# Closings without GpSimd's drain, an earlier gate batch, and experts' weights ahead of the last store

## The chip, the cores and the metric

The kernel runs on one core of a Trainium2 chip, as one program. A core has a matrix engine (TensorE, PE), a vector engine (VectorE, DVE), a scalar engine (ScalarE, ACT), a general one (GpSimd, POOL) and SyncE (SP), which here only issues transfers. The engines run side by side, each in its own order, and wait for one another through semaphores. The metric is the time of one execution on the device, in microseconds, as the median of three runs.

## What is computed

The input `x` is 2 sequences of 4096 tokens with 256 numbers each. Three parts follow one another, each on the result of the last:

```python
x = x + 0.5 * ffn(layernorm(x))        # part one
x = x + attention(layernorm(x))        # part two
x = x + 0.5 * ffn(layernorm(x))        # part three

def ffn(x):                            # 8 experts, each token goes to its best 2
    scores = softmax(x @ gate_w)                       # gate_w: 256 x 8
    scale = the two largest scores of a token, 0 for the other six
    xs = scale.T[:, :, None] * x[None]
    h = silu(xs @ w1[e]) * (xs @ w3[e])                # 256 -> 128
    return sum over e of h @ w2[e]                     # 128 -> 256

def attention(x):                      # 4 heads of 64, chunks of 64 tokens
    q, k, v = silu(causal convolution of x @ Wq, Wk, Wv, 4 taps); q, k normalized
    per chunk: T = inverse(I + strictly lower part of (beta k) k^T)
               mid = T (beta v) - T (beta k) S^T
               out = q S^T + lower part of (q k^T) mid;   S = S + mid^T k
    return (rms norm of out) @ Wo
```

## The kernel before

There are three blocks, one for each part (`ffn`, `attention`, `ffn`). A block holds one program for each engine. At its end all five engines meet, `clear_semaphores` sets the block's semaphores to zero on GpSimd and lets all engines meet once more, and the next block starts.

**How a feed-forward part works.** Each token's row is written twice into a table in memory, `first_rows`, once in each chosen expert's list. Where in a list it goes is its position: how many earlier tokens chose the same expert. GpSimd writes the rows, 128 at a time, by indirect transfers ("scatters"). Then the lists are read in tiles of 128 rows, multiplied with the expert's weights, and scattered again. Part three has no gate of its own: its gate, the positions, the table of tiles and the first scatters are done inside attention, and so is the loading of the experts' weights (`load_weights`: five transfers on SyncE's queue into `raw_w`, 3 MB). ScalarE and VectorE split these into a high part (L2120, eight instructions) and a low part (L1885, eight instructions) before the block ends.

**How attention works.** It takes 32 steps, each of 128 tokens of both sequences, in a pipeline that is written out by hand: `steps_of` calls each engine's `body(f, g, t, s, u, v)`, in which `f`, `g`, `t`, `s` and `u` are the step that is at the front, at the inverses, at their completion, at the state and output, and at the gate. A step's result is added to the residual `xres` (L1653, which raises `y_read`), stored by SyncE (`store_result`), and its gate products are taken. Four steps make one gate batch `v[0]` of 8 tiles; there are 8 batches, 0 to 7. A batch goes through its stages while `v[1]` is 1, 2, 3 and then 0:

- `gate_pow` on GpSimd (L2148, L2151), which needs the statistics of the batch's last result (`gmv_ready`);
- `gate_norm`, `gate_first`, `gate_second`, `gate_sums` on VectorE (to L1743), which choose the experts;
- `positions` on TensorE (L1373 to L1377), three products that count them;
- `gate_scores`, `gate_row_ends`, `gate_ends`, `gate_places` on VectorE (L1749 to L1789), which make each row's scores and places;
- `load_batch` on SyncE, which reads the batch's rows back from `x_after_attention` into the one buffer `xg`, once they are stored and the batch before is scattered;
- `gate_scatter` on GpSimd (L2159), eight scatters.

Batch 6 is in the stage `v[1] == 3` while step 31, the last, is at its state and output. Batch 7 needs step 31's result and runs after it. When its places are known, VectorE works out the table of tiles (`work_out`) and then the weights' low parts. The lines around the change that set the order on SyncE, VectorE and GpSimd:

```python
hold(stored, 64 * (n + 1)); hold(gscattered, 16 * GB * n)   # load_batch
hold(sq_ready, NS); hold(mid_done[h], NS)                   # load_weights
wait(dve, gscattered, 16 * GB * n)                          # gate_row_ends
pool.wait_ge(grow_part, ...); pool.wait_ge(grow_made, ...); pool.wait_ge(xg_loaded, ...)   # gate_scatter
pool.wait_ge(gmv_ready, 4 * (n + 1))                        # gate_pow
hold(gscattered, 16 * NT)                                   # SyncE, last thing in attention
```

## Time and profile before

| | us |
|---|---|
| three runs | 1544.03, 1541.20, 1538.71 |
| median | 1541.2 |
| the profiled execution's own time | 1542.23 |
| its span (first to last instruction) | 1540.5 |
| part one, to attention's first instruction | 394.6 |
| attention, to part three's first instruction | 890.2 |
| part three | 255.7 |

The span is what the profile shows; the profiled execution took 1.7 us more than that. The three parts' lengths are the distances between the first instructions of SyncE's queue in each (at 394.57 and 1284.79 us). The profile gives for each engine the busy time, and for each instruction its start, its length and what ended the idle time before it. An instruction that is busy on an engine that nobody waits for costs nothing.

### The profile page before, as it was taken

How to read it: one execution, taken by the hardware profiler on the slowest of the kernel's cores; microseconds unless marked ns; L12 is line 12 of the kernel's file. 1: busy time of each engine (PE TensorE's matmuls, PEld its weight loads, DVE VectorE, ACT ScalarE, POOL GpSimd, SP SyncE). 2: the span in 40 equal slices, each digit the busy share in tenths (PEclk: the TensorE clock that was granted, in tenths of full speed). 3: DMA queues.
4: the chain of work that ended last, by engine and by line, in shares of the span. 5: the costliest groups of instructions: out<-in, count | busy, mean ns of one | idle time of the engine just before them, and what ended most of it. 6: DMA issues, size and time to landing. Idle time of an engine off the chain costs nothing. (4 is left out here: it accounts for less than half of the span.)

```text
span 1540.5 us, 38923 instructions
## 1 busy us (share of the span) xinstructions
PE 1281.9 (83%) x12840; PEld 1176.3 (76%) x12840; DVE 1083.6 (70%) x2722; ACT 954.4 (62%) x1948; POOL 965.6 (63%) x1716
## 2 busy tenths in 40 slices
PE   6763995898369999999999999999999723994996
PEld 6662995898358888888888888888888623994996
DVE  6574673576467788889888898898887452773674
ACT  2123672774257787788778787787776423772773
POOL 4773565377246566678777786776867431674466
PEclk7665998899679999999999999999999856997999
DMA  7436984774011121232222322223222265875682
GB/s 216 159 105 175 299 268 167 262 271 140 21 20 42 44 52 44 50 92 65 77 61 62 86 64 81 66 59 83 59 79 57 72 193 166 270 252 210 240 287 73
DMA packets 224034, 196.04 MB, mean 127 GB/s; under 512 B 105556, under 2 KB 186714, under 8 KB 223840
## 3 DMA queue, kind: packets, MB, share of 16 engines
q1 hardware_dynamic: 190560, 117.21, 27.7%
q0 software_dynamic: 24576, 67.94, 12.1%
q10 hardware_dynamic: 8704, 8.39, 1.8%
q8 instruction: 111, 1.82, 0.5%
q14 instruction: 83, 0.68, 0.2%
HBM read 103.68 MB, written 96.10 MB: 130 GB/s over the span
## 5 line engine op out<-in xcount | busy, mean ns | idle before, releaser
L1552 DVE SCALAR_TENSOR_TENSOR raw_w<-attn_raw,taps,raw_w 128x256 f32<-128x256 f32 x576 | 246.2, 490 | 30.0 <-ACT raw_w L1934 29.9
L468 PE MATMUL ffn_both<-ws,ffn_xhi 128*128 x1152 | 204.6, 290 | 0.7 <-issue 0.2
L457 PE MATMUL ffn_both<-ident,ffn_xb 128*128 128x128 f32 x576 | 82.1, 290 | 103.1 <-ACT ffn_xb L753 103.1
L468 PEld LDWEIGHTS ffn_both<-ws,ffn_xhi 128*128 128x128 f32 x1152 | 165.1, 193 | 3.2 <-issue 3.2
L2219 POOL TENSOR_TENSOR attn_inv<-attn_inv,attn_term 64x14 f32<-64x14 f32 (+6 forms) x448 | 132.7, 296 | 35.1
L457 PEld LDWEIGHTS ffn_both<-ident,ffn_xb 128*128 128x128 f32 x576 | 70.0, 149 | 105.5 <-ACT ffn_xb L753 83.6
L2216 POOL TENSOR_TENSOR attn_term<-attn_small,attn_inv 64x14 f32<-64x14 f32 (+6 forms) x448 | 125.0, 279 | 32.6
L1204 PE MATMUL attn_fr<-attn_xhi,wqkv 128*128 128x256 f32 x768 | 139.2, 291 | 3.6 <-ACT attn_bth L1941 2.0
L491 PE MATMUL ffn_yb<-ws,ffn_hhi 128*128 x576 | 118.7, 290 | 6.5 <-DVE ffn_hlo L667 6.2
L1204 PEld LDWEIGHTS attn_fr<-attn_xhi,wqkv 128*128 128x128 f32 x768 | 109.7, 193 | 15.2 <-issue 10.6
L468 PE MATMUL ffn_both<-ws,ffn_xlo 128*128 x576 | 116.3, 284 | 0.0
L830 POOL DMA_INDIRECT second_rows<-ffn_more_rows,ffn_to x64 | 63.1, 985 | 84.7 <-DVE ffn_to L652 68.8
L753 ACT ACTIVATE ffn_xb<-ffn_more_rows 128x256 f32<-128x256 f32 x120 | 62.1, 591 | 85.9 <-DMA ffn_more_rows<-first_rows 50.8
L657 DVE TENSOR_TENSOR ffn_xlo<-ffn_both,ffn_xhi 128x1024 fp32r<-128x1024 f32 x72 | 87.7, 1219 | 37.1 <-ACT ffn_xhi L760 37.1
L662 DVE TENSOR_TENSOR ffn_hid<-ffn_both,ffn_sil 128x512 f32<-128x512 f32 x72 | 49.8, 691 | 89.2 <-ACT ffn_sil L765 89.2
L765 ACT ACTIVATE ffn_sil<-ffn_both 128x512 f32<-128x512 f32 x72 | 43.0, 597 | 91.5 <-PE ffn_both L468 91.5
L491 PEld LDWEIGHTS ffn_yb<-ws,ffn_hhi 128*128 128x128 f32 x576 | 93.5, 190 | 7.7 <-issue 7.7
L760 ACT ACTIVATE ffn_xhi<-ffn_both 128x1024 fp32r<-128x1024 f32 x72 | 73.9, 1026 | 34.0 <-PE ffn_both L457 34.0
L2159 POOL DMA_INDIRECT first_rows<-attn_xg,attn_slots x64 | 69.2, 1082 | 35.0 <-issue 16.5
L468 PEld LDWEIGHTS ffn_both<-ws,ffn_xlo 128*128 128x128 f32 x576 | 90.3, 192 | 0.0
L1934 ACT ACTIVATE raw_w<-attn_raw,taps 128x256 f32<-128x256 f32 x192 | 87.0, 501 | 2.0
L819 POOL DMA_INDIRECT first_rows<-ffn_xb,ffn_slots x64 | 65.5, 1023 | 36.3 <-DVE ffn_xb L642 18.1
(310 smaller groups left out, 3878.2 us busy)
## 6 DMA issues: line engine op xcount, KB each, us to landing
ffn_more_rows<-second_rows SPq DMA_DIRECT2D x56, 259.0 KB
ffn_xb<-second_rows SPq DMA_DIRECT2D x48, 259.0 KB, 4.9
raw_w<-second_rows SPq DMA_DIRECT2D x40, 259.0 KB, 4.0
ffn_more_rows<-first_rows SPq DMA_DIRECT2D x64, 131.0 KB
ffn_xb<-in_L_attn_x_dram SPq DMA_DIRECT2D x8, 1024.0 KB, 5.5
attn_xin<-x_after_first ACTq DMA_DIRECT2D x32, 256.0 KB, 2.7
attn_xres<-x_after_first SPq DMA_DIRECT2D x32, 256.0 KB, 3.0
x_after_attention<-attn_xres SPq DMA_DIRECT2D x32, 256.0 KB, 2.2
```

The source lines that it names most:

```text
L457: last = pe.transpose(tr[:, q, j * P:(j + 1) * P], xs[:, k % 2, j, q * P:(q + 1) * P], ident[:])
L468: last = pe.matmul(hp[:, j, :], (xhi, xlo)[b][:, k % 2, q, j * P:(j + 1) * P], ws[:, bass.ds(experts[j], 1), a, q].rearrange("p o d -> p ( ...
L491: last = pe.matmul(yb[:, j, :], (hhi, hlo)[b][:, k % 2, j * P:(j + 1) * P], ws[:, bass.ds(experts[j], 1), a, 2].rearrange("p o d -> p (o d)"),
L657: dve.tensor_tensor(xlo[:, k % 2], tr, xhi[:, k % 2].bitcast(F32), ALU.subtract).then_inc(xlo_ready, 1)
L760: act.activation(xhi[:, k % 2], tr, ACT.Copy).then_inc(xhi_ready, 1)
L819: pool.indirect_dma_start(out=rows1, out_offset=bass.IndirectOffsetOnAxis(ap=slots[:, m % 2, j:j + 1], axis=0), in_=xb[:, m % 4, j, :], in ...
L1204: last = pe.matmul(out, w[:, a, q, col], (xhi, xlo)[b][:, q, :], skip_group_check=True, start=(start and k == 0 and q == 0), stop=(k == 2 ...
L1552: dve.scalar_tensor_tensor(acc[:, j, r], raw[:, j, r, :, tap:tap + P], taps[:, j, r, tap:tap + 1], acc[:, j, r], ALU.mult, ALU.add)\
L1934: act.activation(acc[:, j, r], raw[:, j, r, :, 0:P], ACT.Copy, scale=taps[:, j, r, 0:1])\
L2159: pool.indirect_dma_start(out=rows1, out_offset=bass.IndirectOffsetOnAxis(ap=slots[:, j:j + 1], axis=0), in_=xg[:, j, :], in_offset=None). ...
L2216: pool.tensor_tensor(term[:, 0:k, 0:j], n[:, j + 1:, j:j + 1].broadcast_to([BP, k, j]), v[:, j:j + 1, 0:j].broadcast_to([BP, k, j]), ALU.m ...
L2219: pool.tensor_tensor(v[:, j + 1:, 0:j], v[:, j + 1:, 0:j], term[:, 0:k, 0:j], ALU.subtract)\
```

## The change

Three things are changed.

1. All blocks are opened with `no_gpsimd_drain=True`. GpSimd's `DRAIN` before the meeting at a block's end is gone, at all three blocks. What `clear_semaphores` does between blocks stays: there GpSimd still has a `DRAIN` (L96) before it clears the semaphores, and another before the second meeting (L97). After the last block there is no `clear_semaphores`.
2. Batches 6 and 7 put their counts into `fr` instead of `sc` (`counts_of`). Batch 6's positions stand first in step 31 on TensorE, its places on VectorE behind `remainder`, its load on SyncE one step earlier (`v[1] == 2`), and all its scatters on GpSimd in step 31: two ahead of `out_factor`, six behind it. Batch 7 keeps its place.
3. `load_weights` stands ahead of the last `store_result`.

In the diff the engines follow one another in this order: SyncE, TensorE, VectorE, GpSimd.

```diff
-        block = ctx.enter_context(nc.Block())
+        block = ctx.enter_context(nc.Block(no_gpsimd_drain=True))
...
+        LAST = NS // 4 - 1
+
+        def counts_of(n):
+            a, b = 2 * GB * E, 2 * (GB + 1) * E
+            place = fr[:, 0] if n >= LAST - 1 else sc[:, 1, 2 * E:]
+            return place[:, 0:a], place[:, a:b]
...
-                if v and v[1] == 3:
+                if v and v[1] == (2 if v[0] == LAST - 1 else 3):
                     load_batch(v)
+                if s and isinstance(s[0], int) and (s[0] == NS - 1):
+                    load_weights()
                 if s:
                     store_result(s)
                 if g:
                     collect_inverses(g)
                     place_inverses(g)
-                if s and isinstance(s[0], int) and (s[0] == NS - 1):
-                    load_weights()
...
             def positions(v, u):
                 n = v[0]
                 pe.wait_ge(gmask_ready, n + 1)
-                if u is None:
-                    pe.wait_ge(glg_read, NS)
...
+                if n >= LAST - 1:
+                    pe.wait_ge(vtok_ready, NS)
+                if n == LAST:
+                    pe.wait_ge(grow_part, ROWS * n - 4)
+                each, total = counts_of(n)
...
             def body(f, g, t, s, u, v):
+                if v and v[1] == 3 and v[0] == LAST - 1:
+                    positions(v, u)
                 if s:
                     state_in(s, v)
...
-                if v and v[1] == 3:
+                if v and v[1] == 3 and v[0] != LAST - 1:
                     positions(v, u)
...
             def gate_products_out(u, v):
-                if v and v[1] == 3:
+                if v and v[1] == 3 and v[0] != LAST - 1:
                     dve.wait_ge(gpos_done, v[0] + 1)
...
                 if s:
                     remainder(s)
+                if v and v[1] == 3 and v[0] == LAST - 1:
+                    gate_ends(v)
+                    gate_scores(v)
+                    gate_row_ends(v)
+                    gate_places(v)
...
-                if v and v[1] == 0:
+                if v and v[1] == 0 and v[0] < LAST - 1:
                     gate_scatter(v, 0, 3)
...
-                if v and v[1] == 1 and (v[0] > 0):
+                if v and v[1] == 1 and 0 < v[0] < LAST:
                     gate_scatter((v[0] - 1, 1), 3, 5)
-                if v and v[1] == 2 and (v[0] > 0):
+                if v and v[1] == 2 and 0 < v[0] < LAST:
                     gate_scatter((v[0] - 1, 2), 5, GB)
+                if v and v[1] == 3 and v[0] == LAST - 1:
+                    gate_scatter(v, 0, 2)
                 if s:
                     out_factor(s)
+                if v and v[1] == 3 and v[0] == LAST - 1:
+                    gate_scatter(v, 2, GB)
```

On GpSimd, from step 30's last work to the end of attention, the rows before stand like this (`ws<-ws,attn_cc` is the state's remainder scaled, `attn_og` is `out_factor`, `attn_gvar` and `attn_grstd` are batch 7's `gate_pow`; the first three scatters are batch 5's, the rest are batch 6's and 7's):

```order
L2245 TENSOR_TENSOR ws<-ws,attn_cc 128x256 x2
L2159 DMA first_rows<-attn_xg,attn_slots 67584x262 x3
L2253 TENSOR_TENSOR attn_og<-attn_osum,attn_powers 128x8
L2245 TENSOR_TENSOR ws<-ws,attn_cc 128x256 x2
L2253 TENSOR_TENSOR attn_og<-attn_osum,attn_powers 128x8
L2159 DMA first_rows<-attn_xg,attn_slots 67584x262 x3
L2148 TENSOR_SCALAR attn_gvar<-attn_gmv 128x8
L2151 TENSOR_TENSOR attn_grstd<-attn_gvar,attn_powers 128x8
L2159 DMA first_rows<-attn_xg,attn_slots 67584x262 x13
```

And in the changed kernel, in the same place:

```order
L2258 TENSOR_TENSOR ws<-ws,attn_cc 128x256 x2
L2172 DMA first_rows<-attn_xg,attn_slots 67584x262 x3
L2266 TENSOR_TENSOR attn_og<-attn_osum,attn_powers 128x8
L2258 TENSOR_TENSOR ws<-ws,attn_cc 128x256 x2
L2172 DMA first_rows<-attn_xg,attn_slots 67584x262 x2
L2266 TENSOR_TENSOR attn_og<-attn_osum,attn_powers 128x8
L2172 DMA first_rows<-attn_xg,attn_slots 67584x262 x6
L2161 TENSOR_SCALAR attn_gvar<-attn_gmv 128x8
L2164 TENSOR_TENSOR attn_grstd<-attn_gvar,attn_powers 128x8
L2172 DMA first_rows<-attn_xg,attn_slots 67584x262 x8
```

All of batch 6's scatters now stand ahead of batch 7's `gate_pow`, and two of them ahead of step 31's `out_factor`.

On SyncE's queue, from step 30's residual load on, before (`attn_xres<-x_after_first` is a residual load, `x_after_attention<-attn_xres` a store, `attn_xg<-x_after_attention` a batch's load, `raw_w<-in_L_ffn_w_dram` the weights):

```order
L1108 DMA attn_xres<-x_after_first 128x2x256
L1113 DMA x_after_attention<-attn_xres 128x2x256
L1108 DMA attn_xres<-x_after_first 128x2x256
L1120 DMA attn_xg<-x_after_attention 128x4x256 x2
L1113 DMA x_after_attention<-attn_xres 128x2x256
L196 DMA raw_w<-in_L_ffn_w_dram 128x8x128 x4
L198 DMA raw_w<-in_L_ffn_w_dram 128x8x256
L1120 DMA attn_xg<-x_after_attention 128x4x256 x2
```

And in the changed kernel:

```order
L1114 DMA attn_xres<-x_after_first 128x2x256
L1126 DMA attn_xg<-x_after_attention 128x4x256 x2
L1119 DMA x_after_attention<-attn_xres 128x2x256
L1114 DMA attn_xres<-x_after_first 128x2x256
L196 DMA raw_w<-in_L_ffn_w_dram 128x8x128 x4
L198 DMA raw_w<-in_L_ffn_w_dram 128x8x256
L1119 DMA x_after_attention<-attn_xres 128x2x256
L1126 DMA attn_xg<-x_after_attention 128x4x256 x2
```

Batch 6's load moved past one store and one residual load, and the five weight transfers moved past the last store.

On TensorE, from the gate transpose in step 31 to the gate products behind it, before (`attn_sc<-attn_picked,attn_before` and the two rows behind it are batch 6's positions, `attn_ob<-wos,attn_oT` is step 31's output projection, `attn_sc<-ident,attn_xres` a gate transpose and `attn_sc<-attn_gws,attn_gT` gate products):

```order
L1350 MATMUL attn_sc<-ident,attn_xres 128x128 x4
L1446 MATMUL attn_ob<-ident,attn_on 128x128 x4
L1455 MATMUL attn_ob<-wos,attn_oT 128x256 x4
L1362 MATMUL attn_sc<-attn_gws,attn_gT 128x8 x4
L1373 MATMUL attn_sc<-attn_picked,attn_before 128x128
L1375 MATMUL attn_sc<-attn_upto,attn_ones 128x128
L1377 MATMUL attn_sc<-attn_upto,attn_ones 128x16
L1350 MATMUL attn_sc<-ident,attn_xres 128x128 x4
L1362 MATMUL attn_sc<-attn_gws,attn_gT 128x8 x4
```

In the changed kernel these three rows stand at the start of step 31 (`attn_sc<-attn_state,ws` and `attn_ob<-attn_state,ws` are the step's products with the state):

```order
L1337 MATMUL attn_tp<-raw_w,attn_tt 64x64 x8
L1380 MATMUL attn_fr<-attn_picked,attn_before 128x128
L1382 MATMUL attn_fr<-attn_upto,attn_ones 128x128
L1384 MATMUL attn_fr<-attn_upto,attn_ones 128x16
L1399 MATMUL attn_sc<-attn_state,ws 128x128 x4
L1409 MATMUL attn_ob<-attn_state,ws 128x128 x4
```

Batch 6's positions moved ahead of everything that step 31 does on TensorE, and out of the way of step 31's gate transpose.

## Rows read from the trace of the kernel before

**Rows 1.** Stretches: span time, then each engine's busy time, clock and DMA share.
```profile
core 0: us, PE busy (x) PEld busy (x) DVE busy (x) ACT busy (x) POOL busy (x), PEclk, DMA share, GB/s
...
1243.00:1285.00 42.00, 4.09 (x27) 3.67 (x26) 22.34 (x71) 6.83 (x10) 19.65 (x18) 0.54 0.64 186
```
**Rows 2.** Timeline of GpSimd (POOL), attention's last steps: start us, length us, instruction, [idle before].
```profile
1234.00 1.64 POOL L2253 TENSOR_TENSOR attn_og<-attn_osum,attn_powers 128x8 f32<-128x8 f32 x1 [3.55 <-DVE attn_osum L1636]
...
1245.66 1.06 POOL L2159 DMA_INDIRECT first_rows<-attn_xg,attn_slots  x1 [10.02 <-DVE attn_xg L1789]
...
1249.29 0.27 POOL L2148 TENSOR_SCALAR attn_gvar<-attn_gmv 128x8 f32<-128x8 f32 x1
...
1256.76 0.96 POOL L2159 DMA_INDIRECT first_rows<-attn_xg,attn_slots  x1 [0.30 <-issue]
...
1266.18 0.96 POOL L2159 DMA_INDIRECT first_rows<-attn_xg,attn_slots  x1 [8.46 <-DMA attn_xg<-x_after_attention]
...
1277.09 0.96 POOL L2159 DMA_INDIRECT first_rows<-attn_xg,attn_slots  x1 [0.30 <-issue]
```
**Rows 3.** Timeline of VectorE (DVE), the same stretch.
```profile
1233.04 0.69 DVE L1633 TENSOR_REDUCE attn_oms<-attn_on 128x8 f32<-128x512 f32 x1 [3.40 <-ACT attn_on L2038]
...
1242.03 0.69 DVE L1653 TENSOR_TENSOR attn_xres<-attn_ob,attn_xres 128x512 f32<-128x512 f32 x1 [3.87 <-PE attn_ob L1455]
...
1243.94 0.29 DVE L1774 TENSOR_TENSOR attn_row<-attn_sc,ends 128x128 f32<-128x128 f32 x1 [1.22 <-PE attn_sc L1377]
...
1245.36 0.74 DVE L1660 BATCH_NORM_STATS2 attn_gstats<-attn_xres 128x6 f32<-128x256 f32 x2
...
1259.62 0.17 DVE L1761 TENSOR_SCALAR attn_xg<-attn_xg 128x8 f32<-128x8 f32 x1 [3.22 <-DMA first_rows<-attn_xg,attn_slots]
...
1261.13 0.17 DVE L1789 COPY attn_xg<-attn_slot 128x8 f32<-128x8 f32 x1
...
1268.53 7.03 DVE L1885 TENSOR_TENSOR ws<-raw_w,ws 128x768 fp32r<-128x768 f32 x8
```
**Rows 4.** Timeline of TensorE (PE), the same stretch.
```profile
1228.02 1.16 PE L1392 MATMUL attn_sc<-attn_state,ws 128*128 128x128 f32 x8
...
1243.09 0.47 PE L1373 MATMUL attn_sc<-attn_picked,attn_before 128*128 128x128 f32 x2
...
1256.91 0.45 PE L1377 MATMUL attn_sc<-attn_upto,attn_ones 128*128 128x16 f32 x2
```
**Rows 5.** Timeline of SyncE's queue (SPq), the same stretch.
```profile
1242.75 0.36 SPq L1113 DMA_DIRECT2D x_after_attention<-attn_xres  x1
...
1243.22 4.18 SPq L196 DMA_DIRECT2D raw_w<-in_L_ffn_w_dram  x4
...
1259.68 0.92 SPq L1120 DMA_DIRECT2D attn_xg<-x_after_attention  x2
```
**Rows 6.** Timeline of ScalarE (ACT), the same stretch.
```profile
1256.73 5.97 ACT L2120 ACTIVATE ws<-raw_w 128x768 fp32r<-128x768 f32 x8 [2.60 <-DMA raw_w<-in_L_ffn_w_dram]
```
**Rows 7.** DMA traffic from 1243 to 1257 us.
```profile
DMA packets 5748, 4.21 MB, mean 301 GB/s; under 512 B 182, under 2 KB 5558, under 8 KB 5747
```
**Rows 8.** GpSimd's drains at the closings: count, ns min/median/max, first and last start.
```profile
L893 POOLq DRAIN  x1: 14049/14049/14049, 1269.3 to 1269.3; - x1
...
L224 POOLq DRAIN  x2: 9879/9916/9953, 383.0 to 1530.4; - x2
...
L96 POOLq DRAIN  x2: 178/205/232, 393.2 to 1283.6; - x2
```
**Rows 9.** Who SyncE's queue waited for, from 1530 us on: us in total, times, longest.
```profile
SPq L224 <- PEq L224: 3.4, 1, 3.4
```
**Rows 10.** Timeline, the last scatter of part one and the first instruction of attention.
```profile
387.33 0.98 POOL L830 DMA_INDIRECT x_after_first<-raw_w,ffn_to  x1 [0.30 <-issue]
...
394.57 0.39 SPq L1180 DMA_DIRECT2D attn_gws<-in_L_ffn_gate_w_dram  x1
```
**Rows 11.** Chain that ended last, its first piece: start us, us, what.
```profile
1284.79 0.30 SPq L345
```

More of the change, by code:

```diff
@@ L1057, in attention @@
                              "gscl_ready", "gpos_done", "grow_part", "grow_made", "xg_loaded", "gscattered"))
-        block = ctx.enter_context(nc.Block())
+        block = ctx.enter_context(nc.Block(no_gpsimd_drain=True))
         x_v = src.rearrange("(s n p) d -> n p s d", s=2, p=P)
@@ L1369, in positions @@
                 pe.wait_ge(gmask_ready, n + 1)
[L1370 to L1375 removed]
+                if n >= LAST - 1:
[3 more added lines that the diff above has]
+                each, total = counts_of(n)
+                pe.matmul(each, before[:], choice.rearrange("p r j e -> p r (j e)"),
+                          start=n >= LAST - 1, stop=False, skip_group_check=True)
+                pe.matmul(each, ones[:], upto8[:, :, GB - 1:2 * GB - 1].rearrange("p r j e -> p r (j e)"),
                           start=False, stop=True, skip_group_check=True)
[L1377 removed]
+                pe.matmul(total, ones[:], upto8[:, :, 2 * GB - 1, :],
                           start=False, stop=True, skip_group_check=True).then_inc(gpos_done, 1)
@@ L1770, in gate_ends @@
                 n = v[0]
-                a, b = 2 * E + 2 * GB * E, 2 * E + 2 * (GB + 1) * E
+                each, total = counts_of(n)
                 dve.wait_ge(gpos_done, n + 1)
                 wait(dve, grow_part, ROWS * n)
-                dve.tensor_tensor(row[:], sc[:, 1, 2 * E:a].rearrange("p (r j e) -> p r j e", r=2, e=E),
+                dve.tensor_tensor(row[:], each.rearrange("p (r j e) -> p r j e", r=2, e=E),
                                   kept.ends[:].unsqueeze(2).broadcast_to([P, 2, GB, E]), ALU.add).then_inc(grow_part, 1)
                 dve.wait_ge(grow_part, ROWS * n + 1)
-                dve.tensor_tensor(kept.ends[:], kept.ends[:], sc[:, 1, a:b].rearrange("p (r e) -> p r e", r=2), ALU.add)\
+                dve.tensor_tensor(kept.ends[:], kept.ends[:], total.rearrange("p (r e) -> p r e", r=2), ALU.add)\
                    .then_inc(grow_part, 1)
@@ L1847, in body @@
                     conv(f, 2, 1, 2)
-                if v and v[1] == 3:
+                if v and v[1] == 3 and v[0] != LAST - 1:
                     gate_scores(v)
@@ L1855, in body @@
                     gate_first(v)
-                if v and v[1] == 3:
+                if v and v[1] == 3 and v[0] != LAST - 1:
                     gate_row_ends(v)
@@ L1866, in body @@
                         clear_buffers()
-                if v and v[1] == 3:
+                if v and v[1] == 3 and v[0] != LAST - 1:
                     gate_ends(v)
```

5 lines of the change are left out of this document (removed).

## Prediction

> **What bounds the kernel now.** I read the stretches first, then the timeline of each engine in the one stretch where all are slack, then the drains, and last the chain.
>
> From 1243 to 1285 us TensorE is busy for 4.1 of 42 us and no other engine for much more than half [rows 1]: this is the seam between attention and part three, and nothing there is limited by arithmetic. Its order is read from GpSimd's timeline. Step 31's result is written at 1242.03 + 0.69 = 1242.7 [rows 3]. Batch 6's places follow it, because its positions stand behind step 31's products on TensorE (1243.09, rows 4); they start at 1243.94 on VectorE [rows 3], and the first scatter of batch 6 starts at 1245.66 [rows 2]. Batch 7's `gate_pow` stands behind three of these scatters and starts at 1249.29, though the statistics it needs (0.74 us from 1245.36, and 0.25 us of aggregation) were there at 1246.4 [rows 2, 3]. The last scatter of batch 6 ends at 1257.72 and has landed at 1259.62, when VectorE goes on after 3.22 us of idle time [rows 2, 3]: 1.9 us from issue to landing. Only then can batch 7's rows be loaded into `xg` (1259.68, rows 5), and its scatters run from 1266.18 to 1277.09 + 0.96 = 1278.05, after 8.46 us of waiting for that load [rows 2]. VectorE, with the table and the weights' low parts, is done at 1268.53 + 7.03 = 1275.56 [rows 3], which is sooner. So the seam ends by this: places of batch 6, eight scatters, load, eight scatters.
>
> Then comes GpSimd's drain: it begins at 1269.3 and takes 14.05 us, so it ends at 1283.35, 5.3 us after the last scatter's issue [rows 2, 8]. Part three starts at 1284.79 [rows 11]. At the end of part one the same drain ends at 383.0 + 9.95 = 392.95, 4.6 us after the last scatter's 388.31, and attention starts at 394.57 [rows 8, 10].
>
> **The seam, batch 6.** Its positions cost 0.7 to 0.8 us on TensorE (1243.09 to the next transpose) and now stand ahead of step 31's first products at 1228.02 [rows 4]. That step is a chain from end to end, so all of it moves by +0.8. On VectorE the twelve instructions of places and scores take about 2.3 us (six of them take 1.4, from 1243.94 to the 1245.36 of the next; rows 3); they lie in the 3.40 us in which VectorE waited ahead of 1233.04 [rows 3], and hide there with 1 us to spare. If they did not fit, the excess would be added to the chain. The places are there at about 1232.8, and the rows are loaded since the step before, so the first two scatters run from 1233.1, at 1.3 us each (0.96 and an idle 0.30, rows 2), to 1235.5. `out_factor` stands behind them. It started at 1234.00 [rows 2], would now start at 1234.8, and starts at 1235.5: +0.7 more. Step 31's result is late by 1.5 us: 1244.2. This is what is paid.
>
> What is bought: the other six scatters run behind `out_factor` (ends 1237.2) while TensorE and VectorE finish step 31, 6 x 1.27 = 7.6 us, to 1244.8; landed 1246.7. The statistics of batch 7 need the result and step 30's gate products and are there at 1246.0, 0.4 us sooner than before in spite of the later result, since places no longer stand between. GpSimd is free by then, so `gate_pow` starts at 1246.1, not at 1249.29: -3.2.
>
> **The seam, batch 7.** From `gate_pow`'s start to the end of the positions it was 1249.29 to 1256.91 + 0.45 = 1257.36, 8.1 us [rows 2, 4]; so 1254.2 now. Scores hide beside the positions, and the 3.22 us wait for batch 6's landing goes, as that is over at 1246.7. What follows took 1259.62 to 1261.13 + 0.17 = 1.7 us [rows 3]: places at 1255.9, 5.4 sooner than before.
>
> The scatters also need the rows. The weights are now issued as soon as step 31's middle products are done, about 1232.1 instead of 1243.22. Before, their last byte was there at 1256.73, 13.5 us after the first issue [rows 5, 6], in a stretch that moved 4.21 MB at 301 GB/s [rows 7]. That stretch held eight scatters too, and holds them again, so I take 13.5 us: 1245.6. The last store is issued at 1244.3, finds the end of the weights ahead of it and lands at about 1247; the load of batch 7 then takes what it took, 1259.68 to 1266.18 = 6.5 us [rows 2, 5]: 1253.5, 2.4 us ahead of the places. So the places decide. Scatters start at 1256.2 and take 11.9 us as before (1266.18 to 1278.05): 1268.0.
>
> VectorE's table takes 1261.30 to 1268.53 = 7.2 and the low parts 7.03 [rows 3]: from 1255.9 to 1270.1. ScalarE's high parts, 5.97 us [rows 6], lie ahead of that. So VectorE now reaches the meeting last.
>
> The Trainium skill has a rule against this edit ("DMA: Bandwidth & Descriptors", Queues, rings and completion order): a completion's increment lands only after all earlier writes of the same transfer engine, so a store behind 3 MB of loads is reported behind them. By it the store is there after the weights, as in my sum, and it costs nothing as long as the load wins against the places.
>
> **The drain.** Between blocks GpSimd has another drain, L96, which took at most 0.23 us right behind the long one [rows 8]. What the long one waits for no row says. I bound it from both sides. If it waits for a state that comes 5.3 us (4.6 in part one) after the last scatter's issue, L96 now waits for it: 1268.0 + 5.3 = 1273.3 at the seam. From L96's end (1283.6 + 0.23) to part three's start it was 0.96 us [rows 8, 11]; so part three starts at 1274.3, 10.5 us sooner. At part one's end L96 ended at 393.4 and now ends at 392.95: -0.45. If instead the drain is a routine of 4.6 to 5.3 us that runs when it is called with scatters behind it, it starts only when all engines have met: at the seam 1270.2 + 5.3 + 0.96 = 1276.5 (-8.3), at part one's end 389.9 (some 3 us before the drain's end, where SyncE arrives, as in rows 9) + 4.6 + 1.15 = 395.7 (+1.1). If L96 costs 0.2 whatever came before, 1271.4 (-13.4) and -3.2. I take the first: it lies between the others, and it is what the long drains did, which all began before the last scatters and ended 4.6 to 5.3 us after the last issue.
>
> At part three's end nothing of the kernel follows. SyncE waited 3.4 us for the drain there [rows 9]; that less the meeting is 3.2 us off the span. Whether it is off the time depends on what lies in the 1.7 us between span (1540.5) and time (1542.23), which the trace doesn't show. Ends 0 and -3.2; nothing is nearer to either, and I take the middle, -1.6.
>
> By the Trainium skill ("Runtime: NRT & Kernel Launch", The ~15µs preamble/postamble breakdown) the runtime's own closing waits for all engines. If the time includes it and GpSimd is still held there, this term is 0 and the sum -10.95; no row shows it.
>
> Sum: -10.5 - 0.45 - 1.6 = -12.55. The profiled execution's 1542.23 becomes 1529.7. It lies 1.0 above the runs' median of 1541.2, so the forecast is 1528.6.
>
> **Rivals.**
> - *The drain goes altogether* (L96 costs 0.2): -13.4 - 3.2 - 3.2 = -19.8, 1521.4. For it: it was 0.2 us where it stood. Against: it stood behind the long one.
> - *The drain starts when called*: -8.3 + 1.1 - 1.6 = -8.8, 1532.4. For it: a scatter's bytes are there 1.9 us after issue, and the drain goes on for 3 us more. Against: nothing else.
> - *The weights hold the last batch back.* All transfers of SyncE share one queue. From the point where batch 7's rows land later than 1256.2, each microsecond of delay of the weights is one of the seam; that is weights landed later than 1248.3, 16.2 us after their first issue instead of 13.5. At 20 us it would cost 3.8: 1532.4. At 3.2 MB in 36 us (90 GB/s, where the stretch before had 301 in all) rows land at 1276, scatters end at 1288 against 1278.05, part three starts 9.3 late, and with the other two terms the kernel is slower than before: +7.3, 1548.5. For it: the weights now share the queue with the store that the batch waits for, and with batch 6's scatters. Against: they shared it with these before, at 301 GB/s.
> - *No gain*: the scatters in front of `out_factor` find rows or places missing and GpSimd holds step 31. Each microsecond there is one of the chain; 12 would be needed. The rows are issued 18 us ahead, so this is small.
>
> **How the numbers follow.** My forecast 0.50, the drain gone 0.15, the drain when called 0.17, weights a few microseconds late 0.10, no gain 0.05, slower 0.03. All but the last two are faster by over 0.3% (4.6 us), which is about what a measurement of this kernel can tell from no change: faster 0.91, same 0.06, slower 0.03. The range takes in the drain's two other ends: 1521.5 to 1534.5; what is above it is no gain, slower, and part of the late weights.
>
> **What would show it.** In the new trace: batch 6's first scatter near 1233, `gate_pow` near 1246, batch 7's scatters from 1256 to 1268 with idle time before them put down to the places and not to the load, VectorE's low parts to 1270, and the first instruction of part three at 1274 to 1275 from the span's start (0.45 less with part one's gain). L96's drain shows which of the three it is: ending 5.3 us after the last scatter, lasting 5 us from the meeting, or 0.2. Step 31's result should be 1.5 us later; if it is 3 us later, the cover on VectorE or GpSimd was wrong. If batch 7's scatters wait for the load, the third rival is right.

## The result, and the profile after

| | median of the runs | runs | ratio to before, 95% interval |
|---|---|---|---|
| before | 1542.6 us | 4 (1538.7 to 1548.1) | |
| changed | 1522.3 us | 4 (1519.4 to 1528.7) | 0.9869 [0.9844, 0.9894] |
| changed, a second time on another chip (before there: 1541.6) | 1526.2 us | 5 (1524.4 to 1528.7) | 0.9904 [0.9886, 0.9921] |

The change makes the kernel faster by 20.3 us in the first comparison and by 15.5 us in the second; both intervals lie below 1, and they overlap. A third comparison, on a slower chip (a2 below), gives 0.9904 as well. Medians are of all runs and ratios of the fast ones alone, so the two can differ by some tenths of a per cent (in e1 below the ratio is 0.9922, the medians give 0.995). The forecast was 1528.6 us in a range of 1521.5 to 1534.5: both medians lie in the range, below the forecast. The profiled execution took 1521.02 us with a span of 1519.3; before it was 1542.23 and 1540.5, so the time outside the span is 1.7 us in both.

The drains first, from what the profile tells of lines 96 and 224 (count, ns min/median/max, first and last start). They answer to [rows 8].

```profile
L96 POOLq DRAIN  x2: 173/194/216, 387.3 to 1264.8; - x2
...
L224 SPq DRAIN  x2: 7/7/7, 387.0 to 1519.0; - x2
```

GpSimd's long drains are gone, three of them, and L96's drain, which the forecast let take over their wait, lasts 0.17 to 0.22 us as before. It begins at 387.3 at part one's end, where the last scatter had ended at 385.53, and at 1264.8 at the seam. SyncE's wait in the last closing, 3.4 us before [rows 9], is now 0.2 us:

```profile
SPq L224 <- PEq L224: 0.2, 1, 0.2
```

The timeline around part one's end (start us, length us, instruction, [idle before]), beside [rows 10]: from the last scatter's end to attention's first instruction it is 3.0 us where it was 6.26.

```profile
384.55 0.98 POOL L830 DMA_INDIRECT x_after_first<-raw_w,ffn_to  x1 [0.30 <-issue]
...
388.54 0.39 SPq L1186 DMA_DIRECT2D attn_gws<-in_L_ffn_gate_w_dram  x1
```

At the seam, GpSimd's timeline, beside [rows 2]:

```profile
1227.82 1.06 POOL L2172 DMA_INDIRECT first_rows<-attn_xg,attn_slots  x1 [1.54 <-DVE attn_xg L1797]
...
1230.16 1.69 POOL L2266 TENSOR_TENSOR attn_og<-attn_osum,attn_powers 128x8 f32<-128x8 f32 x1
...
1240.64 0.25 POOL L2161 TENSOR_SCALAR attn_gvar<-attn_gmv 128x8 f32<-128x8 f32 x1 [1.25 <-DVE attn_gmv L1672]
...
1250.72 1.09 POOL L2172 DMA_INDIRECT first_rows<-attn_xg,attn_slots  x1 [8.08 <-DVE attn_xg L1797]
...
1261.26 1.44 POOL L2172 DMA_INDIRECT first_rows<-attn_xg,attn_slots  x1 [0.30 <-issue]
```

Batch 6's first scatter now starts ahead of `out_factor` (L2266), `gate_pow` (L2161) finds GpSimd free and waits 1.25 us for its statistics, and the profile puts the 8.08 us before batch 7's first scatter down to VectorE's places (L1797), no longer to the load. The two end almost together: the places are written at 1249.98 + 0.17 = 1250.15, and 6.41 us lie between the load's issue (1244.31) and this scatter, where it was 6.50 with the load last (1259.68 to 1266.18, rows 2 and 5). VectorE, SyncE's queue and ScalarE in the same stretch, beside [rows 3, 5, 6]:

```profile
1238.25 0.69 DVE L1662 TENSOR_TENSOR attn_xres<-attn_ob,attn_xres 128x512 f32<-128x512 f32 x1 [4.74 <-PE attn_ob L1462]
...
1249.98 0.17 DVE L1797 COPY attn_xg<-attn_slot 128x8 f32<-128x8 f32 x1
...
1257.44 7.03 DVE L1898 TENSOR_TENSOR ws<-raw_w,ws 128x768 fp32r<-128x768 f32 x8
```
```profile
1227.11 4.18 SPq L196 DMA_DIRECT2D raw_w<-in_L_ffn_w_dram  x4
1231.33 2.06 SPq L198 DMA_DIRECT2D raw_w<-in_L_ffn_w_dram  x1
...
1238.97 0.37 SPq L1119 DMA_DIRECT2D x_after_attention<-attn_xres  x1
...
1244.31 0.92 SPq L1126 DMA_DIRECT2D attn_xg<-x_after_attention  x2
```
```profile
1245.37 5.96 ACT L2133 ACTIVATE ws<-raw_w 128x768 fp32r<-128x768 f32 x8
```

The weights are issued 11.9 us ahead of the store. The store of step 31 is issued at 1238.97; the load of batch 7's rows leaves at 1244.31, when it has landed. ScalarE's high parts no longer wait for weights. Scatters end at 1262.70 and VectorE's low parts at 1264.47, so both reach the meeting together (a scatter's landing takes 1.9 us more), and the chain enters part three here, beside [rows 11] (start us, us, what):

```profile
1266.00 0.31 SPq L345
1266.50 0.37 SPq L366
```

The two profiled executions differ by 21.2 us. They are cut here at the same events, each length from the two timelines. One of the cuts is step 30's result, since all that the change moves inside attention, but for batch 6's load, lies behind it. It is the end of these VectorE rows, before and after:

```profile
1225.90 0.69 DVE L1653 TENSOR_TENSOR attn_xres<-attn_ob,attn_xres 128x512 f32<-128x512 f32 x1 [1.20 <-PE attn_ob L1455]
```
```profile
1221.05 0.69 DVE L1662 TENSOR_TENSOR attn_xres<-attn_ob,attn_xres 128x512 f32<-128x512 f32 x1 [1.98 <-PE attn_ob L1462]
```

| stretch | before | after | difference |
|---|---|---|---|
| start to part one's last scatter's end | 388.31 | 385.53 | -2.8 |
| to attention's first instruction (closing) | 6.26 | 3.01 | -3.25 |
| to step 30's result | 832.02 | 833.20 | +1.2 |
| to the last `gate_pow` | 22.70 | 18.90 | -3.8 |
| to batch 7's first scatter | 16.89 | 10.08 | -6.8 |
| to its last scatter's end | 11.87 | 11.98 | +0.1 |
| to part three's first load, L366 (closing) | 7.23 | 3.80 | -3.4 |
| to the kernel's last scatter's end | 250.35 | 251.08 | +0.7 |
| to the end of the span (closing) | 4.87 | 1.72 | -3.15 |

The first, the third and the eighth row are code that the change does not touch: they differ by up to 3 us, which is the spread of single executions. What the change touches sums to -20.3; that this is also the difference of the medians is chance.

### The profile page after: what moved, and what is told of

Its sections match the earlier page's. It is cut to its first block and busy times, and to the rows that moved or that the text cites. A ratio compares the mean times of both kernels' runs of the same rounds, so it can differ in the third digit from the quotient of the medians.

```text
span 1519.3 us, 38931 instructions
## 1 busy us (share of the span) xinstructions
PE 1290.4 (85%) x12840; PEld 1185.1 (78%) x12840; DVE 1084.5 (71%) x2722; ACT 954.0 (63%) x1948; POOL 964.6 (63%) x1716
## 5 line engine op out<-in xcount | busy, mean ns | idle before, releaser
L1210 PEld LDWEIGHTS attn_fr<-attn_xhi,wqkv 128*128 128x128 f32 x768 | 109.5, 193 | 15.6 <-issue 10.6
L2172 POOL DMA_INDIRECT first_rows<-attn_xg,attn_slots x64 | 70.0, 1093 | 26.2 <-issue 16.5
```

The lines of the kernel that those rows point to most:

```text
L1210: last = pe.matmul(out, w[:, a, q, col], (xhi, xlo)[b][:, q, :], skip_group_check=True, start=(start and k == 0 and q == 0), stop=(k == 2 ...
```

## Experiments

Twelve runs were made, of nine kernels, in three groups, each group on one chip with its own runs of the kernel before. The first two groups ran on chips on which the kernel before takes 1676 and 1668 us. The time is lost in the two expert parts: from 200 to 380 us they move 199 to 200 GB/s there where the chips of the first comparison move 223 to 225, and attention takes about as long as before. The third group ran on a chip of the faster kind (1541.6). The seam is read from the timelines, from `gate_pow` on or from step 30's result on, since that is unaffected by the parts' lengths.

**e1_drain_only**: the kernel before, and only this twice:

```diff
-        block = ctx.enter_context(nc.Block())
+        block = ctx.enter_context(nc.Block(no_gpsimd_drain=True))
```

> The kernel before with its blocks opened without GpSimd's drain, and nothing else. Theory A (the drain's whole wait is gone, since the drain behind it, L96, costs 0.2 us on its own): from the last scatter's end to the next part's first instruction 3.0 us at the end of part one (before 6.3) and about 3.4 at the seam (before 6.7), the last closing 3.2 shorter; 9.8 us less than before in all. Theory B (what the long drain waits for is now waited for by L96, as I forecast): L96 lasts 3 us or more, and the time falls by 2 us at most.

Measured: 1667.9 us, ratio 0.9922 [0.9892, 0.9952]. L96's drain is 0.2 us in both places:

```profile
L96 POOLq DRAIN  x2: 173/194/216, 453.0 to 1342.9; - x2
```

The three closings are 3.0, 3.9 and 1.8 us. The theory that L96 takes the wait over is refuted: it lasts 0.2 us and not 3.

**e2_drain_back**: the changed kernel with that edit undone.

> The changed kernel with GpSimd's drain back at all three closings. Theory A: the drain ends 5.3 us after the last scatter's end again and the three closings cost 9.8 us more than in the changed kernel; against before what is left is the seam's order, 9 to 10 us less. Theory B: within 2 us of the changed kernel. A third reading, that the 2.8 us by which part one's last scatter came sooner in the changed kernel's profile belong to the change, would show them here and in the drain-only kernel in every profile; I expect them to differ from profile to profile, as no instruction of part one ahead of its closing was changed.

Measured: 1662.7 us, 0.9928 [0.9896, 0.9961]. The seam's drain ends at 1330.3 + 12.8 = 1343.1, 5.3 us after the last scatter (1337.82), as it did before. Part one's last scatter ends at 450.3 to 453.8 us in this group's four traces, so the 2.8 us there in the first comparison are spread:

```profile
L893 POOLq DRAIN  x1: 12779/12779/12779, 1330.3 to 1330.3; - x1
```

**e3_weights_behind**: the changed kernel with the weights' load behind the last store again.

```diff
-                if s and isinstance(s[0], int) and (s[0] == NS - 1):
-                    load_weights()
                 if s:
                     store_result(s)
...
                     place_inverses(g)
+                if s and isinstance(s[0], int) and (s[0] == NS - 1):
+                    load_weights()
```

> The changed kernel with the experts' weights behind the last store again. Theory A (the weights ahead of the store keep batch 7's load from standing behind 3 MB): the store lands sooner by some 3 us, but the load of batch 7 is issued behind the weights, lands 13.5 to 15 us after the store's issue, and batch 7's scatters wait for it and start 3 to 5 us later; time 3 to 5 us above the changed kernel. Rival (the move hurts: the store lands behind the weights and this holds batch 7): time equal or lower than the changed kernel's.

Measured: 1661.8 us, 0.991 [0.9878, 0.9941]; the time does not tell it from its neighbours. Its timeline does. SyncE's queue and GpSimd:

```profile
1312.41 4.92 SPq L196 DMA_DIRECT2D raw_w<-in_L_ffn_w_dram  x4
...
1319.22 2.58 SPq L1126 DMA_DIRECT2D attn_xg<-x_after_attention  x2
```
```profile
1329.63 1.09 POOL L2172 DMA_INDIRECT first_rows<-attn_xg,attn_slots  x1 [14.41 <-DMA attn_xg<-x_after_attention]
```

SyncE issues the weights for 6.7 us, so batch 7's load leaves at 1319.22, and the scatter that waits for it starts 10.4 us later, among 3 MB of weights. That is 17.7 us after the store's issue (1311.94), where 13.5 to 15 had been expected. The places were ready at 1323.94. All of the gain behind `gate_pow` is gone: 16.4 us to the first scatter, as before (16.9), and not 10. The gain ahead of `gate_pow` stays: it starts 1.3 us after step 31's result, as in the changed kernel (1.7), and not 6.6.

**e4_wait_then_drain**: the changed kernel with the drains back, and GpSimd waiting for the landing of its last scatters ahead of them in all three parts (attention's wait is shown; the expert parts wait on `stored` in the same way).

```diff
+            pool.wait_ge(gscattered, 16 * NT)
```

> The changed kernel with the drains back, and on GpSimd a wait for all its scatters' landing ahead of each. Theory C (the drain is long because it starts with scatters under way or queued; once they have landed it costs 0.2 us, as L96 does): the drain starts at the landing, lasts 0.2 us, and the time is that of the changed kernel, within 1 us. Theory D (the closing's drain is a different thing from L96, or has a price of its own of 3 us once GpSimd has sent transfers): it lasts 3 us or more from the landing, and the time is that of the kernel with the drain back, some 10 us above the changed one.

Measured: 1669.6 us, 0.9964 [0.9936, 0.9991]. All scatters have landed when these drains start, and they still take 4.6 to 5.3 us:

```profile
L224 POOLq DRAIN  x2: 4632/4692/4752, 452.5 to 1660.8; - x2
...
L895 POOLq DRAIN  x1: 5287/5287/5287, 1338.3 to 1338.3; - x1
...
L96 POOLq DRAIN  x2: 172/199/226, 457.4 to 1343.8; - x2
```

So the long drain is not a wait for the transfers: with nothing under way it is as long as the 5.3 us by which it outlasted the last scatter's end in e2. Called early it spends part of that time beside the landing. L96 behind it is cheap here, and without it too (e1).

**a2_after_again**: the changed kernel, unedited, beside the next three.

> The changed kernel itself, run a second time so that the other kernels of this call can be read against it. Theory A (the closings and the seam's other edits are separate gains that add): before's kernel with only the drains taken out gave 0.9922 and the change with its drains put back gave 0.9928, so the product is 0.985. Theory B (the gains overlap, as the prediction's weighing had it where another drain takes the wait over): no better than the better of the two, 0.992. In the trace the three closings cost about 3, 3.4 and 1.7 us from the end of the last scatter to the next SyncE instruction or the span's end, and no drain is longer than 0.3 us.

Measured: 1652.2 us, 0.9904 [0.9875, 0.9933]. The product expected if the halves add, 0.985, lies below this interval, but it comes from two ratios that are each uncertain by 0.003, so this doesn't settle it (f1 to f3 do better). Its closings are 3.0, 5.5 and 1.8 us: the middle one is longer than in the first profile, because VectorE's low parts end at 1337.54, 3.5 us after the last scatter.

**e5_last_drain_back**: `nc.Block(no_gpsimd_drain=first_stage)` in the expert parts: the drain stands in the last closing alone.

> The changed kernel with GpSimd's drain put back in part three's closing alone. Theory A (the last closing's wait counts in the time in full): 3.2 us above the changed kernel of this call, ratio to it 1.002, so 0.987 against before where the changed kernel is 0.985; in the trace the span ends 4.9 us after the last scatter, not 1.7. Theory B (what ends the program outside the span hides it): the same time as the changed kernel though its span has grown by the 3.2 us.

Measured: 1649.3 us, 0.9896 [0.9867, 0.9926]. The medians can't tell 3 us. The profiled execution can: its span ends 4.82 us after the last scatter (a2: 1.76), and its time lies 1.76 us above its span (a2: 1.69). In all traces, with the drain and without, time less span is 1.7 to 1.9 us. So the last closing's 3.1 us are in the time in full.

**e6_drain_probes**: the changed kernel with pairs of `pool.drain()` in attention's GpSimd program.

```diff
+            pool.drain()                                   # L2176, 2177, ahead of its first instruction
+            pool.drain()
             link(pool.memset(powers[:, 0, :], 0.5))
...
+                if v and v[1] == 2 and v[0] in (3, 5):      # behind a batch's last scatter
+                    if v[0] == 5:
+                        pool.wait_ge(gscattered, 16 * GB * 5)
+                    pool.drain()
+                    pool.drain()
...
+            pool.wait_ge(gscattered, 16 * NT)               # L2307, 2308, at its end
+            pool.drain()
+            pool.drain()
```

> The changed kernel with eight drains added to GpSimd's program in attention, in pairs: two before its first instruction (all part one's scatters are landed), two right behind batch 2's last scatter, two at batch 4's after all scatters issued so far have landed, two at its end after all 64 have landed. Theory D (a plain drain pays about 4.7 us for what scatters came since the last one, landed or not): first of a pair 8 to 10 us behind batch 2, about 4.7 us at batch 4 and at the end, the second of each pair under 0.3 us, and the first pair at the start costs 4.7 us too, since part one closed without one. Theory E (the price is the closing's place, not the scatters): all eight are under 0.3 us. Theory F (every plain drain has a fixed price of about 4.7 us): second ones cost as much as first ones. By D the end of attention comes 4.7 us later than in the changed kernel.

Measured: 1658.7 us, 0.9946 [0.9922, 0.997].

```profile
L2176 POOLq DRAIN  x1: 34/34/34, 448.6 to 448.6; - x1
...
L2288 POOLq DRAIN  x2: 1354/4215/7076, 979.3 to 1191.6; - x2
...
L2289 POOLq DRAIN  x2: 34/38/41, 986.4 to 1193.0; - x2
...
L2307 POOLq DRAIN  x1: 2007/2007/2007, 1342.3 to 1342.3; - x1
...
L2308 POOLq DRAIN  x1: 34/34/34, 1344.4 to 1344.4; - x1
```

The first of a pair pays, the second takes 0.03 to 0.04 us. But the price is not the fixed 4.7 us of theory D: with everything landed it is 1354 ns at batch 4 (16 scatters since the drain before) and 2007 ns at the end (24 scatters). And the pair at the start costs nothing, though part one closed without a long drain and its 208 scatters were still unpaid by that theory. What stands between is the closing with L96 and L97. L96 itself is the first drain behind those 208 scatters and took 0.2 us, so not every drain pays. Behind batch 2 the drain is called early and ends at 979.3 + 7.08 = 986.4, 3.3 us after the last scatter's end (983.06), where 24 landed scatters cost 2.0; no run explains the 1.3 us between.

**e7_batch6_back**: the changed kernel with batch 6's load, positions, gates and scatters in their old places (the conditions on `LAST - 1` in the four programs taken out, two of them shown).

```diff
-                if v and v[1] == (2 if v[0] == LAST - 1 else 3):
+                if v and v[1] == 3:
                     load_batch(v)
...
-                if v and v[1] == 3 and v[0] == LAST - 1:
-                    gate_scatter(v, 0, 2)
```

> The changed kernel with batch 6 put back: its rows' load, its positions, its gates and its scatters stand where the kernel before has them (batch 7's counts still have their own PSUM place, the weights still load ahead of the last store, and the drains are out). The prediction's step: with batch 6's scatters spread over batch 7's steps again, GpSimd's gate_pow comes about 3 us later behind two scatters, batch 7's places about 5 us later, and the last scatter lands 8 to 10 us later: 5 to 9 us above the changed kernel (0.988 to 0.990 of before). Rival (batch 6's advance does nothing, the rest of the gain came from the weights or the store): within 1 us of the changed kernel.

Measured: 1657.1 us, 0.9948 [0.9923, 0.9973], 4.8 us above a2; the two intervals overlap, so here too the timeline decides. SyncE's queue and GpSimd:

```profile
1317.61 0.92 SPq L1126 DMA_DIRECT2D attn_xg<-x_after_attention  x2
```
```profile
1324.22 0.96 POOL L2165 DMA_INDIRECT first_rows<-attn_xg,attn_slots  x1 [8.26 <-DMA attn_xg<-x_after_attention]
```

The load of batch 7's rows is held until batch 6's late scatters have landed, 10.1 us after `gate_pow` (a2: 4.4), and the scatters wait for it. `gate_pow` starts 6.1 us after step 31's result again (a2: 1.3). This is the old seam, with the weights long there.

**e8_drain_forms**: the changed kernel with the drains back and probes ahead of them: in parts one and three two `pool.drain()` ahead of the closing's own (in part one behind a wait for the landing), at the seam a wait for the landing and 30 memsets, and between part one and attention two empty blocks with one memset each. Only the first of these edits is shown.

```diff
+            if first_stage:
+                for b in range(NW):
+                    pool.wait_ge(stored[b], 16 * TPB * ((NST + NW - 1 - b) // NW))
+            pool.drain()                                   # L867
+            pool.drain()                                   # L868
```

> The changed kernel with the closings' drains put back and probes before them. Part one's closing: GpSimd waits for all stores of part one, then two drains of its own, then the closing's drain. Between part one and attention: two empty blocks with a memset each, so two closing drains with nothing scattered since the semaphore clear. Seam: GpSimd waits for the landing of all scatters, then some 7 us of memsets, then the closing's drain. Part three's closing: two drains right behind the last scatter, then the closing's drain. Theory G (the first drain after scatters pays, whichever it is, once): part one's and part three's closing drains are under 0.3 us behind probes of 2 to 5 us, both empty blocks' drains under 0.3 us, the seam's drain still 4.7 to 5.3 us. Theory H (the closing's drain is a dearer form, whatever came before): all of them, the empty blocks' too, cost 4.6 to 5.3 us. Theory I (what is paid is time since the last scatter, so waiting hides it): the seam's drain falls under 0.3 us behind 7 us of memsets. Its time is not compared: it is some 10 to 20 us above the changed kernel by its added waits.

Measured in a single execution: 1548.1 us. Parts one and three first, then the empty blocks' closings (L2327), then the seam: GpSimd's memsets and the drain behind them.

```profile
L867 POOLq DRAIN  x2: 4648/7240/9831, 388.7 to 1536.2; - x2
...
L868 POOLq DRAIN  x2: 41/112/183, 393.7 to 1546.0; - x2
...
L225 POOLq DRAIN  x2: 34/34/34, 393.9 to 1546.1; - x2
...
L2327 POOLq DRAIN  x2: 262/264/266, 395.1 to 395.6; - x2
```
```profile
1275.85 7.79 POOL L2308 MEMSET probe<- 128x128 f32 x30 [1.72 <-DMA first_rows<-attn_xg,attn_slots]
```
```profile
L899 POOLq DRAIN  x1: 5537/5537/5537, 1283.4 to 1283.4; - x1
```

Theory G holds for the closing's drain and for the kernel's own, but not for "whichever it is": L96 in e1 is an exception. The first drain behind the scatters takes 4648 ns with all landed, or runs until 4.7 us after the last scatter when it is called early (1536.2 + 9.83 = 1546.0, last scatter's end 1541.35). The second takes 0.04 to 0.18 us, and the closing's own only 34 ns behind them. The empty blocks' drains take 0.26 us. The seam's drain starts at 1283.4, 7.5 us after the landing (1275.85), and takes 5.54 us all the same, so what is paid does not pass with time (theory I is out), and it isn't a dearer form (H is out).

**f1_after, f2_drain_only, f3_drain_back**: the changed kernel, e1's and e2's kernels again, on one chip of the faster kind.

> The changed kernel once more, beside the two halves of the change on one chip. Theory A (the halves add): its ratio to before is the product of the two others', near 0.985. Theory B (they overlap): it is no better than the better of the two by more than 0.1%, about 0.991. The trace's stretch from the last gate_pow to batch 7's last scatter is 20.5 to 22 us.

> The kernel before with the drains taken out of the three closings and nothing else (as in the earlier run of it, 0.9922). Theory A: 9.8 us below before, three closings of 3.2 to 3.3 us each, ratio 0.994 at some 1670 us. Theory B: 3.7 us below before, the middle closing alone.

> The changed kernel with the three drains put back (as in the earlier run of it, 0.9928). Theory A: the seam's gain alone, 8 to 9 us below before, ratio 0.995. Theory B: 13 to 16 us below before, since the drain hides behind the wait for scatters once the seam is shorter.

| | median | ratio to before (1541.6) |
|---|---|---|
| f1, both halves | 1526.2 | 0.9904 [0.9886, 0.9921] |
| f2, drains out alone | 1534.3 | 0.995 [0.9931, 0.9969] |
| f3, the seam alone | 1530.3 | 0.9922 [0.9904, 0.994] |

The halves give 7.4 and 11.4 us, together 18.7, and the whole gives 15.5. That f1's ratio should be 0.985 was wrong: 0.9904 is nearer to the 0.991 of theory B, while f2 came as expected (0.994), and f3 lies between its two theories. Within the intervals the halves still add. The traces show how much is lost. From step 30's result to part three's first load it is 58.7 us before, and 54.6 and 55.9 with the drain out (e1, f2), so the drain is worth 2.8 to 4.1 us at the old seam. With both edits of the seam it is 46.6 and 47.5 with the drain (e2, f3) and 44.8 to 45.4 without it (changed, a2, e5, f1), so it is worth 1.2 to 2.7 there. The reason is VectorE. In f3 the way from the last scatter's end (1265.11) to part three's load (1272.34) is 7.2 us, GpSimd's drain being last; in f1 it is 5.5 (1263.89 to 1269.43), and not the 3.8 of f2, because VectorE's low parts end later than the scatters:

```profile
1260.37 7.03 DVE L1898 TENSOR_TENSOR ws<-raw_w,ws 128x768 fp32r<-128x768 f32 x8
...
1269.43 6.72 SPq L366 DMA_DIRECT2D ffn_more_rows<-first_rows  x12
```

They end at 1267.40; L96's drain starts at 1267.7, and part three's load 2.03 us after the low parts' end, as in the first profile (1264.47 to 1266.50), a2 and e5. In the first profile the scatters took 12.0 us and not 10.6, so that both ended together; in f1, a2 and e5 VectorE alone is last, and 1.7 us of the drain's 3.4 are given to it.

VectorE doesn't explain why the second comparison gives 15.5 us and the first 20.3. What the change touches, cut as in the table above, sums to -20.2 in f1's profile against the first profile of the kernel before, and from `gate_pow` to part three's load the two have the same 25.9 us. No trace of the kernel before was taken on that chip. The intervals overlap, and the cause of the difference is open.

All seams in one table, in us: step 31 from step 30's result to its own, then to the last `gate_pow`; and from this `gate_pow` to batch 7's first scatter, to its last scatter's end, and to part three's first load:

| kernel | batch 6 early | weights ahead | drain | step 31 | to `gate_pow` | first | last | part three |
|---|---|---|---|---|---|---|---|---|
| before | no | no | yes | 16.1 | 6.6 | 16.9 | 28.8 | 36.0 |
| e1, f2 | no | no | no | 16.1, 16.1 | 6.3, 7.5 | 16.7, 16.5 | 28.4, 28.5 | 32.3, 32.3 |
| e7 | no | yes | no | 16.1 | 6.1 | 16.7 | 28.5 | 32.9 |
| e3 | yes | no | no | 17.1 | 1.3 | 16.4 | 28.5 | 32.2 |
| e2, f3 | yes | yes | yes | 17.2, 16.9 | 1.7, 1.3 | 9.9, 10.8 | 20.5, 22.0 | 27.7, 29.3 |
| changed, a2, e5, f1 | yes | yes | no | 17.2, 16.9, 16.8, 17.2 | 1.7, 1.3, 2.0, 1.7 | 10.1, 11.0, 10.5, 9.8 | 22.1, 21.6, 21.1, 20.4 | 25.9, 27.1, 26.6, 25.9 |

Behind `gate_pow` either edit of the seam without the other gives nothing; both give 5 to 8 us. Each alone leaves batch 7's rows late: without the first the buffer is free too late, without the second the load queues behind the weights. But batch 6 early also moves `gate_pow` itself, with the weights ahead or not. So from step 30's result to batch 7's first scatter it is 39.0 to 40.1 us with neither edit, 39.0 with the weights alone, 34.8 with batch 6 alone, and 28.7 to 29.3 with both: batch 6 alone brings about 5 us, the weights alone nothing, and the weights bring 5 to 6 more once batch 6 is early.

## Why the prediction came out right, and where not

The number came out inside the range because the range had been stretched to take in the drain's other two ends; the forecast's own sum had the drain wrong. Its part of the seam ahead of the closings was right: from step 30's result to batch 7's last scatter's end -10.5 us were measured and -10.05 (1278.05 to 1268.0) forecast. The three closings gave -9.8 where -2.5 was forecast. Together that is -20.3 instead of -12.55.

*Batch 6 early.* Right in its mechanism and nearly in its sizes. The first scatter ran at 1227.82 ahead of `out_factor`. Step 31 took 17.20 us and not 16.13, so it paid 1.1 (forecast 1.5): 0.7 on TensorE, where the positions stand in front (forecast 0.8), and 0.4 at `out_factor` (forecast 0.7); VectorE's places were hidden, as it is 3.4 us from the subtraction at L1625 to L1642, as before. Counted from step 30's result, `gate_pow` came 3.8 us sooner (forecast 3.2) and the places 6.3 (forecast 5.4). Other runs say the same: step 31 takes 16.1 us in all four traces without the edit and 16.8 to 17.2 in all with it, and `gate_pow` follows its result after 6.1 to 7.5 us without and 1.3 to 2.0 with it. Counted from attention's first instruction this is hard to see, since `gate_pow` lies anywhere from 847.5 to 861.3 us (869.9 in e6, with drains inside attention): that spread arises ahead of step 31.

*Batch 7, "so the places decide".* It came out as a tie. Both edits are needed to get there, as the table shows. That the load would win by 2.4 us was wrong in size: the weights landed 16.2 us after their first issue, not 13.5, which is the very point at which the third rival was to decide. They were issued 5.4 us after step 30's result, as forecast (5.5), the store landed 1.0 us behind them, and from the load's issue to the first scatter it was 6.4 us (forecast 6.5). In a2, e5 and f1 the scatter starts 0.3 us after the places, so these decide; in f3 it starts 1.3 us after them and the load was last (1247.32 to 1253.90). That rival's worst case, 90 GB/s, rests on no row; 3 MB in 16.2 us is about 190. By its own terms it makes part three 9.5 us late and not 9.3, and the listed chances of a faster kernel sum to 0.92 and not 0.91.

*VectorE.* "VectorE now reaches the meeting last" was right: it is alone in f1, a2 and e5, and level with the scatters in the first profile.

*The weights ahead of the store.* The Trainium skill ("DMA: Bandwidth & Descriptors", Queues, rings and completion order) has the store's report behind the writes that lie ahead of it. The trace agrees in order, store landed at 1244.27 and weights at 1243.3, and the store's landing takes 5.3 us where it had taken 2.4; no run separates the rule from plain sharing of the engines.

*The drain: this step failed.* The forecast let L96 take the wait over, ending 5.3 us after the last scatter. L96 waited for nothing of the kind and lasted 0.2 us. The reason given, that the long drains "all began before the last scatters and ended 4.6 to 5.3 us after the last issue", is a fact about the drain and was read as one about the scatters. The first rival, "the drain goes altogether", was right in all its terms: the closings gave 3.25 us at part one's end (forecast 0.45), 3.4 at the seam (forecast 0.4: 1274.3 less 1268.0 is 6.3, where it had been 6.74) and 3.15 at the end (forecast 1.6). Its 1521.4 us is nearest to the first result (1522.3). The second comparison (1526.2) lies between it and the forecast; why is open (see f1).

*The last closing.* The middle of 0 and -3.2 was taken, with no row for either end; it is the whole, by e5. The sentence from the Trainium skill ("Runtime: NRT & Kernel Launch", The ~15µs preamble/postamble breakdown), by which GpSimd might still be held in the runtime's closing, would have made it 0: no run shows any sign of that, as time less span is 1.7 to 1.9 us with the drain and without.

## What to carry to other kernels

A drain that ends some microseconds after the last transfer isn't shown to wait for it: put the wait for the landing ahead of the drain, and what it still takes is its own price. If every engine that needs the data waits on the transfers' semaphores anyway, that price can go. And where two holds lie on one buffer (its last reader, and the queue that its load stands in), take both away at once: here the rows' arrival behind `gate_pow` moved with neither edit alone and by about 6 us with both. Judge such an edit from an event ahead of everything that it touches: counted from `gate_pow` batch 6's edit alone seems to bring nothing, counted from step 30's result it brings about 5 us.

## What the runs showed of the hardware

- GpSimd's drain pays once for the indirect scatters issued since the drain before it, although they have landed: 1354 ns for 16, 2007 for 24, 5287 and 5537 for 64, which is 83 to 87 ns each. For parts one and three, with 208 and 144 scatters, many of them into other tables, it is 4632 to 4752 ns and so not in proportion; what sets it there is open. Called early, the drain for 64 ends 5.3 us after the last scatter's end, so it runs beside the landing.
- A closing without a long drain leaves nothing to be paid later: the drains behind it (164 to 232 ns for L96's in every kernel, 34 to 45 ns for L97's in e6) were cheap, and so were e6's two at attention's start. Why L96, the first drain behind 208 or 64 scatters there, pays nothing is open; whether the clearing settles the scatters in another way was not tried.
- One program on several chips of one kind: 1541 to 1543 us on two, 1668 and 1676 on two others, the difference in the parts where the DMA engines are busiest.
- Not run: in the changed kernel GpSimd is idle for 8 us ahead of batch 7's scatters, while VectorE's eight low parts (7.03 us, L1898) are last at the seam in a2, e5 and f1. Two of them on GpSimd would take up to the 1.7 us named above, an estimate that leaves out what they would cost there; in the first profile, where both end together, they would give nothing.
